# Second attention of a four-block kernel: row maxima carried in the query strips, one matmul pass for transposed scores, causal mask of the natural scores added by VectorE in the PSUM bank

## What is computed

```python
nx = _layernorm(x, ln1_w, ln1_b)
qkv = nx @ Wqkv + bqkv            # 16 heads of 16
scores = jnp.einsum('bqhd,bkhd->bhqk', q, k) / jnp.sqrt(jnp.float32(HEAD_DIM))
scores = jnp.where(causal, scores, jnp.finfo(scores.dtype).min)
attn = jax.nn.softmax(scores, axis=-1)
out = jnp.einsum('bhqk,bkhd->bqhd', attn, v).reshape(B, S, D)
x = x + out @ Wo + bo
```

## Time and profile before

| what | value |
|---|---|
| median of three runs | 1744.22 us |
| the profiled execution's own time | 1746.09 us |
| its span | 1744.2 us |
| PE busy in the span | 1620.8 us (93%) |
| VectorE busy | 1146.9 us (66%) |
| ScalarE busy | 899.1 us (52%) |
| granted TensorE clock, mean | 0.972 of full |

### The profile page before, as it was taken

How to read it: one execution, slowest core, us unless ns; L and a number is a source line. 1 busy time by engine, 2 the same in 40 slices (tenths; PEclk the granted TensorE clock), 3 DMA queues, 4 the chain that set the end, 5 groups by cost and what they waited for, 6 DMA issues and landing times.

```text
span 1744.2 us, 32605 instructions
## 1 busy us (share of the span) xinstructions
PE 1620.8 (93%) x11293; PEld 1109.7 (64%) x11294; DVE 1146.9 (66%) x2716; ACT 899.1 (52%) x1970; POOL 378.7 (22%) x447
## 2 busy tenths in 40 slices
PE   8998989889999877999998889999999999989998
PEld 6555545445555565999995444665666666567887
DVE  4776767656555377444445778877766776867776
ACT  2887878635555543444443557756665665720000
POOL 1111111322453221111111321432323231210000
PEclk9999999989999978999998999999999999999999
DMA  8787778543233164556563311100100010020001
GB/s 299 262 289 258 253 260 289 185 66 60 46 58 64 54 217 146 201 192 205 199 211 102 91 41 34 55 13 25 36 24 27 13 31 25 2 85 1 1 0 48
DMA packets 89023, 194.72 MB, mean 112 GB/s; under 512 B 10592, under 2 KB 53216, under 8 KB 84416
## 3 DMA queue, kind: packets, MB, share of 16 engines
q1 hardware_dynamic: 85488, 183.75, 33.6%
q0 software_dynamic: 3408, 9.31, 1.7%
HBM read 129.19 MB, written 51.25 MB: 103 GB/s over the span
## 4 chain that ended last, share of the span: by engine, by line
PE 79%; DVE 10%; ACT 6%; issue 3%; DMA 1%; DVEq 0%; SPq 0%; POOL 0%; ACTq 0%; POOLq 0%
PE PS L1555 10%; PE PS L1391 8%; PE PS L1510 6%; PE PS L973 5%; PE PS L1426 5%; PE PS L1525 5%; PE PS L1500 5%; PE PS L1374 4%; PE PS L1040 4%; PE PS L1062 3%; PE PS L1481 3%; PE PS L1151 2%; PE PS L1073 2%; PE PS L1376 2%; PE PS L1123 2%
## 5 line engine op out<-in xcount | busy, mean ns | idle before, releaser
L1984 ACT ACTIVATE P<-PS,nm 128x512 f32<-128x512 f32 x256 | 174.6, 695 | 108.5 <-DVE nm L2592 87.3
L1510 PEld LDWEIGHTS PS<-idf,P 128*128 128x128 f32 x1024 | 118.0, 143 | 101.9 <-issue 69.9
L2185 DVE CUSTOM_DVE_ANT_0 SN<-PS,SR 128x128 f32<-128x128 f32 (+3 forms) x256 | 115.4, 488 | 92.8 <-PE PS L1044 92.7
L1510 PE MATMUL PS<-idf,P 128*128 128x128 f32 x1024 | 155.9, 282 | 15.5 <-ACT PTb L1994 13.9
L2247 DVE TENSOR_REDUCE mxs<-PS 128x2 f32<-128x512 f32 (+3 forms) x128 | 105.5, 824 | 96.7 <-PE PS L1137 96.4
L2592 DVE TENSOR_REDUCE nm<-PS 128x2 f32<-128x1024 f32 x128 | 150.4, 1215 | 24.7 <-PE PS L1500 23.9
L1391 PE MATMUL PS<-xT,W1c 128*128 128x128 f32 x1248 | 145.9, 275 | 2.8 <-ACT xT L1909 1.8
L1391 PEld LDWEIGHTS PS<-xT,W1c 128*128 128x128 f32 x1248 | 142.6, 192 | 5.0 <-ACT xT L1909 2.3
L1843 ACT ACTIVATE PTf<-PS 128x1024 f32<-128x1024 f32 (+3 forms) x128 | 89.3, 704 | 87.0 <-PE PS L1125 86.8
L1726 ACT ACTIVATE SN<-SN,nm 128x128 f32<-128x128 f32 (+3 forms) x256 | 128.8, 555 | 7.0 <-DVE nm L2185 6.9
L2812 DVE SCALAR_TENSOR_TENSOR X<-PS,gat,X 128x256 f32<-128x256 f32 x224 | 97.0, 479 | 46.2 <-PE PS L1555 45.3
(11 more groups left out here) (364 smaller groups left out, 3577.7 us busy)
## 6 DMA issues: line engine op xcount, KB each, us to landing
W1c<-in_fc1T SPq DMA_DIRECT2D x39, 1024.0 KB, 5.3
SR<-rel SPq DMA_DIRECT2D x16, 1024.0 KB, 7.7
rel<-EN SPq DMA_DIRECT2D x15, 1024.0 KB, 4.8
SR<-rel SPq DMA_DIRECT2D x16, 768.0 KB, 6.8
rel<-EN SPq DMA_DIRECT2D x15, 768.0 KB, 4.3
SR<-rel SPq DMA_DIRECT2D x16, 512.0 KB, 4.2
W2f<-in_fc2T SPq DMA_DIRECT2D x8, 1024.0 KB, 8.1
rel<-EN SPq DMA_DIRECT2D x15, 512.0 KB, 3.3
```

The source lines that it names most:

```text
L1510: last = nc.tensor.transpose(TR1[j][:, c * P:c * P + P], P1[s % 4][:, j, c * P:c * P + P], idf[:])
L1984: last = af(P1[s % 4][:, j, :], PD[s % 2][:, j, :], ACT.Exp, bias=nm1[:, s % 4, j:j + 1], accum_out=sm1[:, s % 4, j:j + 1])
L2185: v.tensor_tensor_reduce(SN[k % 6][:, 0:w], SB[k % 3][:, 0:w], SR[r][:, 2 * pr + i, :], -1.0, -LOW, ALU.add, ALU.min, nm[:, k % 16:k % 16 ...
```

## The change

- `row_max` first adds the mask (`maskf`, now f32 in SBUF, made in the first attention) to the last 128 columns of both heads in the bank, waits for that addition, then reduces as before. The two mask matmuls are gone, and `idh` and `maskh` with them. The natural matmuls contract over 48 partitions (DQ), so that they don't see the maxima.
- The transposed scores take one matmul a head: the maxima lie in rows 48 to 51 of the query strips. `max_strip_rows` on SP copies them there from `MS` with two DMAs a group, after ScalarE's copy; PE's first transposed scores of a group wait for those DMAs (`f_ml`), and ScalarE's copy for the DMAs of two groups before.
- AHEAD is 14 instead of 12, FIRST_G 0 instead of 5, MX_STEP 4 instead of 6; the last block of values moves from step 4 to step 3, `copy_out` from step 4 to 3, POOL's `place_max` before its second select; key projections of a batch take steps 0, 1, 5, 6 instead of 0, 1, 4, 5, query projections steps 0 and 1 with both parts each instead of 0, 1, 4, 5.
- SP's order: keys 2, queries 2, keys 3, maxima 0; then in each group n keys n + 4, queries n + 3, maxima n + 1, with keys that begin a batch behind the maxima.

```diff
-AHEAD = NUF + 4
+AHEAD = NUF + 6
-V_STEPS = {2: (0,), 3: (1, 2), 4: (3,)}
-MX_STEP, OT_STEP = 6, 7
+V_STEPS = {2: (0,), 3: (1, 2, 3)}
+MX_STEP, OT_STEP = 4, 7
-FIRST_G = 5
+FIRST_G = 0
+            def max_strip_rows(n):
+                m_done(sp, ("mx", n))
+                for x in range(2):
+                    rows = slice(HS * x + DQ, HS * x + DQ + DM)
+                    sp.dma_start(QD[n % NQD][rows].bitcast(F32),
+                                 MS[n % 2][rows].bitcast(F32).unsqueeze(1).to_broadcast([DM, 2, S])).then_inc(f_ml, 16)
-            for m in range(2, NJ):
+            for m in (2, 3):
                 key_strips(m)
-                query_strips(m)
-                if m == HGS:
+                if m < NQD - 1:
+                    query_strips(m)
+                else:
+                    max_strip_rows(0)
+            for n in range(NJ):
+                k, q = n + NKD - 1, n + NQD - 1
+                if k < NJ and k % HGS:
+                    key_strips(k)
+                if q < NJ:
+                    query_strips(q)
+                if n + 1 < NJ:
+                    max_strip_rows(n + 1)
+                if k < NJ and k % HGS == 0:
+                    key_strips(k)
+                if n == 0:
                     sp.wait_ge(a_x, NJ)
...
                 for c in range(RT):
-                    if c == 2 and n + 1 < NJ:
+                    if c == 1 and n + 1 < NJ:
                         place_max(n + 1)
...
                     if u == 0:
-                        m_done(pe, ("mx", n))
+                        pe.wait_ge(f_ml, 32 * n + 32)
...
-                        mm(bank(x), keys(x), QD[n % NQD][HS * x:HS * x + HS, t, c * P:S], start=True, stop=False)
-                    for x in range(2):
-                        last = mm(bank(x), keys(x), MS[n % 2][HS * x:HS * x + HS, c * P:S], start=False, stop=True)
+                        last = mm(bank(x), keys(x), QD[n % NQD][HS * x:HS * x + HS, t, c * P:S], start=True, stop=True)
...
-                        mm(NB[:, x, 0:w], QD[m % NQD][HS * x:HS * x + HS, y, r * P:r * P + P],
-                           KD[m % NKD][HS * x:HS * x + HS, y, 0:w], start=True, stop=False, skip_group_check=True)
-                    for x in range(2):
-                        last = mm(NB[:, x, w - P:w], idh[:], maskh[:], start=False, stop=True, skip_group_check=True)
+                        last = mm(NB[:, x, 0:w], QD[m % NQD][HS * x:HS * x + DQ, y, r * P:r * P + P],
+                                  KD[m % NKD][HS * x:HS * x + DQ, y, 0:w], start=True, stop=True)
...
                 bank = m_written(act, ("mx", n))
                 if n >= 2:
-                    act.wait_ge(f_st, (n - 1) * NUF)
+                    act.wait_ge(f_ml, 32 * n - 32)
...
                 dve.wait_ge(f_nat, g + 1)
+                diag = NB[:, :, w - P:w]
+                link(v.tensor_tensor(diag, diag, maskf[:].unsqueeze(1).to_broadcast([P, 2, P]), ALU.add))
                 v.tensor_reduce(mxs[m % 2][:, r, :, y], NB[:, :, 0:w], AX.X, ALU.max).then_inc(f_max, 1)
```

More of the change, by code:

```diff
@@ L58 @@
 H_PARTS = {(0, 2): [(("hv", 0, 0), 0)], (0, 3): [(("hv", 0, 0), 1)], (0, 7): [(("hv", 0, 1), 0), (("hv", 0, 1), 1)],
-           (2, 4): [(("h", 6), 1)], (3, 4): [(("h", 7), 1)]}
+           (2, 5): [(("h", 6), 1)], (3, 5): [(("h", 7), 1)]}
 for _b in range(1, B):
-    for _i, _u, _use in ((4, 0, ("hk", _b, 0)), (4, 4, ("hk", _b, 1)), (3, 0, ("hq", _b, 0)), (3, 4, ("hq", _b, 1)),
-                         (2, 0, ("hv", _b, 0)), (1, 0, ("hv", _b, 1))):
+    for _i, _u, _use in ((4, 0, ("hk", _b, 0)), (4, 5, ("hk", _b, 1)), (2, 0, ("hv", _b, 0)), (1, 0, ("hv", _b, 1))):
         for _p in range(2):
             H_PARTS[4 * _b - _i, _u + _p] = [(_use, _p)]
+    for _x in range(2):
+        H_PARTS[4 * _b - 3, _x] = [(("hq", _b, _x), _p) for _p in range(2)]
 H_WHOLE = {at: [_use for _use, _p in parts if _p == 1] for at, parts in H_PARTS.items()}
@@ L299, in build @@
         kc = place("kc", [P, 2], F32)
-        maskh = place("maskh", [P, P], BF16)
-        idh = place("idh", [P, P], BF16)
+        maskf = place("maskf", [P, P], F32)
         PTf = [[place(f"PTf{i}_{c}", [P, HQ, S - c * P], F32, rPT + 20 * KB * i + KB * c * (9 - c)) for c in range(RT)]
@@ L529, in build @@
         f_mx = sem("f_max_placed")
+        f_ml = sem("f_max_rows_loaded")
         strip_sem = {"k": a_w[0] + [sem("f_keys_loaded4")], "q": a_w[1]}
@@ L1858, in _ @@
                         other_f(use)
-                    if u == 4 and n:
+                    if u == 3 and n:
                         copy_out(n - 1)
@@ L2271, in _ @@
                         dve.wait_ge(s_causal, 2)
-                        v.tensor_copy(idh[:], idf[:])
-                        v.tensor_copy(maskh[:], maskw[:, S - P:]).then_inc(s_bp, 1)
+                        v.tensor_copy(maskf[:], maskw[:, S - P:]).then_inc(s_bp, 1)
                     if (n, u - 2) in FIRST_H:
```

## The result

| | before | after |
|---|---|---|
| median, same chip, 4 runs each | 1746.18 us | 1800.36 us (1798.51 to 1806.48) |
| ratio | 1 | 1.0312 (95%: 1.0274 to 1.035) |
| profiled execution, its span | 1746.09, 1744.2 us | 1799.45, 1797.0 us |
| granted TensorE clock, mean | 0.972 | 0.939 |

The account below looks back on a forecast made before the run. Bound: the loop of PE and VectorE through `NB`, the one pair of natural-score banks. 1746.1 + 30.6 (loop 13.3, start 14.1, end 3.2) + 24 for lost clock - 1.9 = 1799 us; range 1765 to 1840.

Parts of the forecast that it names:

- The circle through `NB`: PE and VectorE alternate on natural-score banks; mask matmuls out, addition in: net +0.24 us a turn, 2.26 at 512 wide.
- Second pass removed: Two transposed-score matmuls a step dropped, 0.24 us at 512 wide; worth nothing where the loop binds.
- Groups at full clock: Attention loop: bare group 14.8 us, values 15.2, keys 15.5, queries 16.4; stretch 218.4 instead of 205.1, +13.3.
- The clock: TensorE falls to 1.2 GHz in sparse steps; 2.3 us a group in 10 or 11 of 14 groups, +24.
- The start: Before the first transposed scores: natural turns delay outputs, constant rows, strips and maxima; scores at 397.9 us, +14.1.
- The tail: After the last natural scores: the last group's maxima lie on the path; +3.2 us.
- SP and landing +8.3: Stage's end: last maxima landed by DMA 8.3 us after the last natural turn, against 4.8 before to first scores.
- Keeps its 11.8: Stage's end: the last group, bound by exp, still takes 11.8 us, less about 0.3.
- Clock kept: Rival: the loop lengthens but the clock stays high; 1776.7 us, or 1775 on the median's footing; chance 0.32.
- Lost in the dense steps too: Rival: low clock also through values and projections, about 6 us a group, 84 in all; 1860 us; chance 0.10.
- Faster: Rival: addition plus wait below 0.21 us, so the period follows PE's issue; 1721 us; chance 0.05.
- the 30 to 55 given as a sign: Sign of being right: the attention stage ends some 30 to 55 us later.

Follow-up runs that it names:

- add_twice: The changed kernel with the mask added twice on VectorE; 1852.73 us, ratio 1.0622.
- aligned_mask_on_pe: mask_on_pe with row blocks reordered so score widths meet the steps of the kernel before, and FIRST_G 5; 1764.59 us, ratio 1.0129.
- mask_on_pe: The changed kernel with the mask matmuls back on PE and no addition on VectorE; 1783.07 us, ratio 1.0216.
- wide_scores: The changed kernel with extra 512-wide pairs of transposed scores on PE as filler, overwritten by the real pair; 1787.1 us, ratio 1.0261.
- aligned_wide: aligned_mask_on_pe with extra 512-wide filler pairs, none in steps next to a projection; 1750.12 us over 12 runs, ratio 1.0018.
- scores_often: The changed kernel with each step's transposed pair issued 1 to 12 times, to fill PE's waits; 1795.17 us, ratio 1.0285.
- halves_one_pass: mask_on_pe with each head's bank of natural scores handed over by itself and two reductions a turn; 1885.66 us, ratio 1.08.

## Why the prediction was right, and which of its terms were off

**The circle through `NB`.** Right. Turn 2.28 against 2.26, addition 0.43 against 0.42, and add_twice shows that it counts in full (0.43 a turn). The Trainium skill (page VectorE: DVE Perf Modes, section The TRN2 errata) has a formula for an f32 tensor_tensor, (N + 151) / 0.96 ns, which it states as exact at N = 512 and 2048. Used at N = 256, which is an estimate from that page, it gives 424 ns, and the mean here is 431. The upper bound of 0.74 for the addition is a slip: by the reductions in the earlier trace rows, 0.27 us for 256 columns, doubling that part gives 0.69. Nothing else was worked out from it.

**Second pass removed.** Right in size, nearly nothing: 0.25 a group in aligned_mask_on_pe. What I left out is that its matmuls are also work that holds the clock; mask_on_pe, which adds nothing to the circle, ran its loop at 0.84. How much of its 17.6 us is clock, how much the step arrangement and how much the waits for the maxima's DMAs (2.4 us) can't be parted exactly, since they act on each other: with the arrangement of before (and FIRST_G 5) 7.1 us go, and with filler another 14.4, which brings the clock to 0.97.

**Groups at full clock.** Right, and none too low. From the turns at a granted 1.00 that the estimate under wide_scores uses, a group with keys takes 15.0 (15.5 forecast), with queries 16.0 (16.4), with values 14.9 to 15.0 (15.2), a bare one some 14.8 (14.8). The loop at full clock comes to some 216 us where 218.4 was forecast: +11 instead of +13.3.

**The clock.** Right that it falls in part and comes back in the dense steps, and nearly right in size. 237.8 - 216 = 22 us in the loop and 3 to 4 in the tail (below) stand where I put 24 in all. It came differently divided: a dozen spells of low clock, of 1.8 us each in the mean, where I counted 10 or 11 of 2.3; they mostly begin in step 6 or 7 and end in step 1 or 2 of the next group, and the groups 4 and 8, whose steps 5 and 6 hold key projections, had none there. The Trainium skill (page TensorE: Matmul & The Clock Gate, HAM oscillation) names long idle gaps as the cause; the trace disagrees, since PE's longest wait for `row_max` in the waits above is 2.0 us and the clock fell in most groups. Another section of that page (A second HAM failure mode: psum-queue depth-cycling) has PE idling briefly between groups of matmuls as a cause of the same; that is what these rows look like, but no run isolates it.

**How near the sum came, and how much of it was luck.** The three stretches that the forecast speaks of grew by 16.9 + 32.6 + 7.4 = 56.9, and 54.6 was forecast: by the estimates here the parts are off by +2.8 (start), -2.5 (loop at full clock), +0.7 (tail at full clock) and +1.3 (clock). The two stretches that the change leaves alone gave +2.1 and -6.2. That 1799 met 1800.36 to 1.4 us is luck; that it lay within a few us is not.

**The start.** The chain was right; the first transposed scores came at 402.80 instead of 397.9. Of these 4.9 us the first natural scores, which started 2.1 later and waited for the query strips, are one part (over the fourteen profiled runs they started between 363.9 and 371.6, so this is scatter and not the change); seven turns of 14.2 instead of 12.9 us another (they ran at the low clock: the 512-wide pairs there take 0.80); SP's three blocks, 12.4 instead of 11.4 (4.72 for the first), 1.0; the maxima's issue and landing, 399.60 to 402.80, 3.2 against 2.9, and 0.2 before POOL's constant rows.

**The tail.** Forecast +3.2, measured +7.4. Most of the 4.2 that were missing is the clock (0.72 in the tail), which these steps did not count. "SP and landing +8.3" became 10.9; among others the 24 matmuls of values that stand on the way to the last maxima took 2.76 us (1.49 in a group at full clock). In wide_scores, whose tail has a granted 1.00, PE was released by the maxima 8.3 us after the last natural matmuls at 628.43, as forecast:

```profile
636.76 0.96 PE L1144 MATMUL PS<-QD,KD 64*128 64x512 f32 x6 [0.21 <-DMA QD<-MS]
```

"Keeps its 11.8" (less 0.3) became 13.1, from 651.52 to 664.57, at a granted 0.77; in aligned_wide it took 12.2 at 1.00, with some filler in it. So at full clock the tail would be some 20.5, +4 instead of +3.2, and 3 to 4 us of it are the clock.

**The rivals.** "Clock kept", 1775, is refuted by 0.79 in the loop. "Lost in the dense steps too", 1860, is not what happened: the stretches with key and query projections ran at a granted 1.00, and in the others the clock came back during the values. "Faster" needed an addition with its wait below 0.21; it is 0.47. Two details of the forecast do not hold: the stage ended 59.0 us later (664.57 against 605.60), outside the 30 to 55 given as a sign, and the upper end of the range is more than its terms give, since 1799 + 20 for the addition and + 8 for the clock in all 14 groups make 1827, not 1840.

## What to carry to other kernels

Before taking a busy engine for the bound, follow the one buffer that two engines pass to and fro: work added inside that circle costs its full time in every turn, work taken out beside it is worth next to nothing. Matmuls that look superfluous in such a loop may be what holds TensorE's clock; removing them can cost more than they took (here 14.4 us of the loop came back with filler, where the removed pass was worth 0.25 a group), so read the granted clock group by group, before and after. A transfer that is covered in one arrangement need not be in the next: the maxima's DMAs cost 0.5 us of the loop here, 4.2 in aligned_wide. Where only the filler is at issue, try it once with wide matmuls to see what the clock is worth.

## What was not expected of the hardware

- Filler of two kinds gave two clocks: PE busy 217.2 of 236.7 us with mostly narrow repeats (scores_often) a granted 0.90, 215.2 of 227.3 with 512-wide pairs (wide_scores) 0.98. Width, number and place of the repeats all differ between the two, so which of them decides isn't shown.
- PE shown busy 317.86 of 318.30 us at a granted 0.62 (halves_one_pass). Its matmuls use half of the array one at a time; whether that is why the clock fell wasn't isolated and stays open.
- Two matmuls on the two halves of the array, issued one behind the other, have an extent of 0.50 us at 512 columns; one alone has 0.50 too.
- An addition in place in a PSUM bank costs what one from PSUM to SBUF does: 431 ns against 0.42 us for the same 128x256.
- The two parts of the change do not add: 32.7 us in the loop for the mask alone, 17.6 for the rest, 32.6 for both (at equal numbers of turns 33, 21 and 36). That the clock had been lost already in both cases (0.87, 0.84, 0.79) fits this; it is an argument and was not tested by itself.
